# An attention block in one pass: the first batch's values multiplied early, the other batches' values from half-precision parts

## The reference

```python
out = bilinear_resize(x, 64, 64)
out = relu(bn(conv1x1(out, conv1_w), bn1_s, bn1_b))
q, k, v = conv1x1(out, q_w, q_b), conv1x1(out, k_w, k_b), conv1x1(out, v_w, v_b)
energy = einsum('bdi,bdj->bij', q, k)            # q, k: 32 channels, 4096 points
out = gamma * einsum('bcj,bij->bci', v, softmax(energy)) + out
out = relu(bn(out, bn2_s, bn2_b))
out = bilinear_resize(bn(conv1x1(out, conv2_w), bn3_s, bn3_b), 128, 128)
return relu(out + x)
```

## Time and profile before

| | us |
|---|---|
| median of 3 runs (2367.70 to 2368.66) | 2367.78 |
| the profiled execution, whole | 2371.97 |
| its span in the trace | 2370.2 |
| first batch: entry until the first product of the blocks | 0 to 144.3 |
| second batch: entry | 624.4 to 708.1 |

### The profile page before, as it was taken

The page is one execution under the profiler, slowest core; times in us unless marked ns, Lnnn a source line. Parts: engine busy times, 40 slices in busy tenths (PEclk is TensorE's granted clock), DMA queues, the critical chain, the costliest instruction groups (busy, mean ns, idle before and its releaser), DMA issues.

```text
span 2370.2 us, 48197 instructions
## 1 busy us (share of the span) xinstructions
PE 2298.5 (97%) x15970; PEld 1650.3 (70%) x15970; DVE 1783.7 (75%) x3294; ACT 1706.3 (72%) x3305; POOL 1671.0 (70%) x1610
## 2 busy tenths in 40 slices
PE   4799999999999999999999999999999999999998
PEld 2377777777667777777747777777775777777774
DVE  7666578887568888888657888888756777777778
ACT  5567777777657777777755777777765777777773
POOL 7992468888369988888728988889845454444464
PEclk8899999999999999999999999999999999999999
DMA  6321112322102332222301322233310112222322
GB/s 212 107 72 46 36 54 107 106 92 104 54 23 103 108 107 103 93 105 98 107 10 54 109 106 102 102 107 106 106 55 1 63 63 71 71 71 71 142 96 100
DMA packets 59273, 204.11 MB, mean 86 GB/s; under 512 B 8752, under 2 KB 9840, under 8 KB 59120
## 3 DMA queue, kind: packets, MB, share of 16 engines
q1 hardware_dynamic: 41696, 138.93, 18.2%
q10 hardware_dynamic: 17424, 63.45, 6.5%
HBM read 135.24 MB, written 67.11 MB: 85 GB/s over the span
## 4 chain that ended last, share of the span: by engine, by line
PE 88%; DVE 4%; ACT 3%; POOL 3%; issue 1%; SPq 1%; DMA 0%; DVEq 0%; ACTq 0%; POOLq 0%
PE acc L1139 19%; PE acc L1141 18%; PE acc L1140 18%; PE et L1015 10%; PE emx L1003 6%; PE wrk L1037 4%; PE acc L1065 4%; PE wrk L1003 3%; PE acc L1057 2%; PE wrk L1028 1%; DVE qs L768 1%; DVE ks L768 1%; PE acc L1049 1%; ACT qs L535 1%; ACT qs L534 1%
## 5 line engine op out<-in xcount | busy, mean ns | idle before, releaser
L1139 PE MATMUL acc<-vh,ph 128*128 128x257 f16 x4096 | 1120.1, 273 | 1.7 <-DVE vl L778 1.4
L1141 PE MATMUL acc<-vh,pl 128*128 128x257 f16 x4096 | 1116.2, 273 | 0.0
L1140 PE MATMUL acc<-vl,ph 128*128 128x256 f16 x4096 | 1110.9, 271 | 0.0
L463 ACT ACTIVATE ph<-et 128x512 f16<-128x512 f32 x1024 | 610.5, 596 | 301.8 <-PE et L1015 293.0
L727 DVE TENSOR_TENSOR pl<-et,ph 128x512 f16<-128x512 f32 x1024 | 700.6, 686 | 139.4 <-ACT et L464 135.8
L464 ACT ACTIVATE et<-et 128x512 f32<-128x512 f32 x1024 | 607.0, 593 | 0.0
L1140 PEld LDWEIGHTS acc<-vl,ph 128*128 128x128 f16 x4096 | 400.9, 98 | 277.4 <-issue 20.5
L1139 PEld LDWEIGHTS acc<-vh,ph 128*128 128x128 f16 x4096 | 400.2, 98 | 70.6 <-issue 11.0
L1141 PEld LDWEIGHTS acc<-vh,pl 128*128 128x128 f16 x4096 | 395.4, 97 | 56.2
L377 POOL TENSOR_TENSOR ct<-cd,uw 128x512 f32<-128x512 f32 x246 | 325.0, 1343 | 134.7 <-DVE xres L758 130.3
L1015 PE MATMUL et<-qs,ks 98*128 (+1 forms) x1024 | 390.2, 381 | 2.7 <-DVE pl L727 0.9
(11 more groups left out here) (142 smaller groups left out, 2673.0 us busy)
## 6 DMA issues: line engine op xcount, KB each, us to landing
xres<-in_x SPq DMA_DIRECT2D x139, 512.0 KB, 4.5
out<-xres ACTq DMA_DIRECT2D x121, 512.0 KB, 2.6
xin<-in_x SPq DMA_DIRECT2D x110, 512.0 KB, 3.7
xr<-in_x SPq DMA_DIRECT2D x7, 512.0 KB, 7.4
out<-xr SPq DMA_DIRECT2D x6, 512.0 KB, 2.6
out<-xr SPq DMA_DIRECT2D x2, 256.0 KB, 2.1
osb<-in_L_conv_conv_w SPq DMA_DIRECT2D x1, 256.0 KB, 7.7
osb<-in_L_conv_v_w SPq DMA_DIRECT2D x1, 256.0 KB, 7.8
```

The costliest lines, as they stand in the source:

```text
L463: ops.activation(ph[:, t % 4, :], et[t % 2][:, :], ACT.Exp)
L1139: mm(acc[it][:, 0:C + 1], ph[:, tt % 4, pt], vh[:, tt, 0:C + 1], start=tt == 0, stop=False)
L1140: mm(acc[it][:, 0:C], ph[:, tt % 4, pt], vl[:, tt, :], start=False, stop=False)
L1141: last = mm(acc[it][:, 0:C + 1], pl[:, tt % 4, pt], vh[:, tt, 0:C + 1], start=False, stop=tt == JT - 1)
```

## The change

In the first batch, v0 to v13 are multiplied between the steps of the convolution: the two values of chunk k-1, v(2k-2) and v(2k-1), stand behind c(2k+1) and the m that follows it. As the scale isn't known yet, ACT copies each result in float32 into `xr`, over rows that the convolution has used (`keep_values`). After q7, ACT makes the eight high parts of 1024 columns each from these copies (`kept_high`), and DVE the low parts: two in the entry, six in the steps 1, 3, 5, 7, 9 and 11 of the first block (`kept_low`). POOL writes a chunk of `xr` for the next batch only after its values were multiplied.

In the other batches the values' operands are split into half-precision parts: ACT and DVE split `a` (scaled) chunk by chunk into `a_high` and `a_low`, again kept in `xr`, and PE multiplies 12 half-precision matmuls for each v. The scale of `a` comes from the size of the batch's small image, which DVE reads in eight reductions in the last block of the batch before (`largest_z`), from sums on PE at step 29, and from constants made once in block 1 (`fixed_sizes`).

```diff
+        def a_part(ck, low, half):
+            return xr[:, ck].rearrange("p h r c -> p (h r c)").bitcast(F16)[:, (low * CH + half) * IB:(low * CH + half + 1) * IB]
+        def kept(ck):
+            return xr[:, ck].rearrange("p h r c -> p (h r c)")
...
 (SP, last block)
-                    sp.wait_ge(c1_rdy, 2 * NB * B)
+                    sp.wait_ge(v_rdy, VU * B)
...
 (POOL, blk)
+                        if j == 0:
+                            pool.wait_ge(v_rdy if b else v_done, b * VU + 2 * (n + 1))
...
 (ACT)
+            def a_high(b, ck):
+                if ck == 0:
+                    act.wait_ge(a_rdy, b)
+                for half in range(CH):
+                    last = ops.activation(a_part(ck, 0, half), a[:, half, ck * IB:(ck + 1) * IB], ACT.Copy,
+                                          scale=a_scale[:, half:half + 1])
+                last.then_inc(a_hi, 1)
+            def keep_values(v):
+                act.wait_ge(v_rdy, v + 1)
+                ops.activation(kept(v // 2)[:, v % 2 * VB * C:(v % 2 + 1) * VB * C], acc[bank_of(0, "values", v)][:, :],
+                               ACT.Copy).then_inc(v_kept, 1)
+            def kept_high(ck):
+                if ck == 0:
+                    act.wait_ge(vscale, 4)
+                act.wait_ge(v_kept, 2 * ck + 2)
+                ops.activation(vh[:, ck * IT:(ck + 1) * IT, 0:C], kept(ck).rearrange("p (j c) -> p j c", c=C), ACT.Copy,
+                               scale=vg[:, 2:3]).then_inc(vh_rdy, 2)
...
 (DVE)
+            def a_low(b, ck):
+                dve.wait_ge(a_hi, (b - 1) * NB + (ck + 1))
+                for half in range(CH):
+                    last = ops.scalar_tensor_tensor(a_part(ck, 1, half), a[:, half, ck * IB:(ck + 1) * IB],
+                                                    a_scale[:, half:half + 1], a_part(ck, 0, half), ALU.mult, ALU.subtract)
+                last.then_inc(a_lo, 1)
+            def largest_z(b, ck):
+                dve.wait_ge(down_p, down_count(b + 1, PIECES * (ck + 1)))
+                ops.tensor_reduce(z_max[:, ck, :], xr[:, ck].rearrange("p h r c -> p h (r c)"), AX.X, ALU.max,
+                                  apply_absolute_value=True).then_inc(z_seen, 1)
+            def kept_low(ck):
+                dve.wait_ge(vh_rdy, 2 * ck + 2)
+                js = slice(ck * IT, (ck + 1) * IT)
+                ops.scalar_tensor_tensor(vl[:, js, :], kept(ck).rearrange("p (j c) -> p j c", c=C), vg[:, 2:3], vh[:, js, 0:C],
+                                         ALU.mult, ALU.subtract).then_inc(v_done, 2)
...
 (PE, values)
+                        if not is_first(b):
+                            high, low = (a_part(jt // IT, i, h)[:, keys] for i in range(2))
+                            mm(out, high, wvh[:, h, :], start=h == 0, stop=False)
+                            mm(out, high, wvl[:, h, :], start=False, stop=False)
+                            last = mm(out, low, wvh[:, h, :], start=False, stop=h == CH - 1)
+                            continue
...
 (PE, step 29 of a batch's last block)
+                        for h in range(CH):
+                            last = mm(wrk[:, C + 1:C + 2], ones_p[:, :], z_all[:, h:h + 1], start=h == 0, stop=h == CH - 1)
+                        last.then_inc(z_sum, 1)
...
+def _first_sequence(engine):
+    seq, kept = [], [("kept", ck) for ck in range(NB)]
+    for ck in range(NB):
+        m = [("max", u) for u in range(IT * (ck - 2), IT * (ck - 1))] if ck >= 2 else []
+        first, second, middle = [("conv1", 2 * ck)], [("conv1", 2 * ck + 1)], [("qk", ck - 1)] if ck else []
+        v = [("values", i) for i in range(2 * ck - 2, 2 * ck)] if ck else []
+        if engine == "V":
+            seq += first + second + m[:3] + middle + m[3:]
+        else:
+            seq += first + m[:2] + middle + m[2:3] + second + m[3:] + v
...
+T_KEPT = (1, 3, 5, 7, 9, 11)
+T_Z = (1, 3, 7, 10, 12, 19, 20, 26)
```

More of the change, by code:

```diff
@@ L552, in enter @@
                         conv1_out(b, i // 2, i % 2)
+                        if i % 2 and not is_first(b):
+                            act.wait_ge(c1_done, b * (2 * NB) + (i + 1))
+                            a_high(b, i // 2)
                         if i == 1 and not is_first(b):
@@ L557, in enter @@
                         qk_high(b, i)
+                    elif kind == "values" and is_first(b):
+                        keep_values(i)
+                    elif kind == "kept":
+                        kept_high(i)
                     elif kind == "values":
@@ L787, in enter @@
                         qk_low(b, i)
+                    elif kind == "a_low" and not is_first(b):
+                        a_low(b, i)
                     elif kind == "max":
@@ L851, in blk @@
                         pair_max(b, n + 1, units[0])
+                    if g == 1 and t == T_FIXED:
+                        fixed_sizes()
+                    if c == NB - 1 and b < B - 1:
+                        if t in T_Z:
+                            largest_z(b, T_Z.index(t))
+                        if t == T_Z[-1]:
+                            size_of_z(b)
+                        if t == T_SIZE + 1:
+                            size_of_a(b)
+                    if g == 0 and t in T_KEPT:
+                        kept_low(2 + T_KEPT.index(t))
                     if c > 0 and t in (T_OT[0] + 1, T_OT[1] + 1):
@@ L1166, in blk @@
                         shift_transposes(g + 1)
+                    if c == NB - 1 and t == T_SIZE and not (isinstance(b, int) and b == B - 1):
+                        pe.wait_ge(y_rdy, g * 2)
+                        pe.wait_ge(z_rdy, b + 1)
+                        for h in range(CH):
+                            last = mm(wrk[:, C + 1:C + 2], ones_p[:, :], z_all[:, h:h + 1], start=h == 0, stop=h == CH - 1)
+                        last.then_inc(z_sum, 1)
+                        if is_first(b):
+                            pe.wait_ge(a_size, 1)
+                            for h in range(CH):
+                                last = mm(wrk[:, C + 2:C + 4], ones_p[:, :], a_parts[:, h, :], start=h == 0, stop=h == CH - 1)
+                            last.then_inc(a_sum, 1)
             def batch(b):
@@ L1217 @@
 PAR_OPS = 5
+def _first_sequence(engine):
[8 more added lines that the diff above has]
+            seq += first + m[:2] + middle + m[2:3] + second + m[3:] + v
+    m = [("max", u) for u in range(EU - 2 * IT, EU)]
+    v = [("values", i) for i in range(VU - 2, VU)]
+    row, one, scale, qk, shift, rows = (("bound_row", 0), ("bound_all", 0), ("scale", 0), ("qk", NB - 1), ("shift", 0),
+                                        ("shift_rows", 0))
+    energies = [("energies", i) for i in range(3)]
+    if engine == "V":
+        return seq + [row, m[0], m[1], one, scale, m[2], qk, *m[3:], kept[0], rows, kept[1], *energies]
+    if engine == "A":
+        return seq + [qk, *v, *kept, *energies]
+    return seq + [m[0], m[1], row, qk, one, m[2], m[3], v[0], m[4], m[5], v[1], m[6], m[7], shift, *energies]
 def _sequence(vector):
@@ L1227, in _sequence @@
         first, second, middle = [("conv1", 2 * ck)], [("conv1", 2 * ck + 1)], [("qk", ck - 1)] if ck else []
-        seq += first + second + m[:3] + middle + m[3:] if vector else first + m[:2] + middle + m[2:3] + second + m[3:]
+        low = [("a_low", ck - 1)] if ck else []
+        seq += first + second + m[:3] + middle + m[3:] + low if vector else first + m[:2] + middle + m[2:3] + second + m[3:]
     m = [("max", u) for u in range(EU - 2 * IT, EU)]
@@ L1232, in _sequence @@
     if vector:
-        seq += [row, m[0], m[1], one, scale, m[2], qk, v[0], m[3], m[4], m[5], v[1], m[6], v[2], m[7], *v[3:6]]
+        seq += [row, m[0], m[1], one, scale, m[2], qk, v[0], m[3], m[4], m[5], v[1], m[6], v[2], m[7], ("a_low", NB - 1), *v[3:6]]
     else:
@@ L1247, with ring_of, bank_of @@
 A_SEQUENCE.insert(A_SEQUENCE.index(("qk", NB - 1)) + 1, ("values", 0))
[L1248 removed]
+FIRST_SEQUENCE, V_FIRST, A_FIRST = (_first_sequence(e) for e in "PVA")
+FIRST_RING, RING = ([x for x in q if x[0] in ("conv1", "qk", "values")] for q in (FIRST_SEQUENCE, SEQUENCE))
 assert [RING.index(("values", VU - IT + i)) % IT for i in range(IT)] == list(range(IT))
[L1252 to L1253 removed]
+def ring_of(b):
+    return FIRST_RING if isinstance(b, int) and b == 0 else RING
+def bank_of(b, kind, i):
+    return ring_of(b).index((kind, i)) % 4
 AHEAD = 3
```

114 lines of the change are left out of this document (91 added, 23 removed).

## The result

The changed kernel takes 2386.8 us (median of 4 runs, 2384.0 to 2388.5) against 2368.2 (4 runs, 2367.7 to 2368.7): a ratio of 1.0073, 95% interval 1.0061 to 1.0086, some 17 us slower. The forecast was 2375.0, in a range of 2360 to 2384. The direction was right, and the size was off by more than half.

What follows compares the result with a forecast made beforehand. PE bounds the kernel, busy 2298.5 of 2370.2 us, except in the first batch's head, a chain of load, ACT, DVE and PE. First batch +6.4, later batches −1.3, constants +2.2: +7.3 on 2367.78 gives 2375.0 us, range 2360 to 2384.

Steps and rivals of the forecast that it cites:

- The head: First batch's entry: ACT's copies delay the weighted rows, turns of 15.5 us instead of 11.8, c14 at 117.3.
- the 2.5: First batch's head: a stop of PE lowers its clock and costs 2.5 us beyond itself.
- A: The forecast itself: head turns of 15.5 us, clock falling at stops; 2375.0 us, range 2369 to 2382; chance 0.47.
- B: First batch's head: same circle of waits, but the clock stays up, turns of 13.0 us; 2365 us; chance 0.22.
- ACT's high parts: End of the first batch's entry: eight high parts of 1024 columns, 1.03 us each, 8.3 us in all.
- block 0's loss of clock: Start of block 0: PE stands over 6 us before it, so the low clock costs 2.5 us.
- The gain of the tail: Later batches, v7 to v15: half-precision values save 0.41 us for each of nine units, 3.7 us per batch.
- The failed step: Convolution of batches 1 to 3: splits fit DVE's idle 2.5 us per chunk, meeting POOL at odd chunks; +0.6 per batch.
- D: Convolution of later batches: DVE's low parts wait for POOL, 1.1 us per chunk, 22 us, taken as +13; 2388; chance 0.12.
- fixed_sizes: Block 1, step 2: 3.8 us of DVE work between two differences that PE waits for; +2.2 us (0 to 4).
- largest_z: Last block of the batch before: eight reductions of 1.3 us hidden in 15 us of DVE idle time; without cover 10.
- C: Head: copies don't hold up weighted rows, loads come late and POOL alone sets c14 at 101.4; 2359 us; chance 0.13.

Runs made afterwards that it cites:

- e9: Changed kernel with ACT's copies behind the weighted rows, fixed_sizes split over three steps, last two chunks' low parts later in DVE's queue; ratio 0.9950 to before.
- e3: Changed kernel without DVE's low parts in batches 1 to 3, PE multiplying the high part in their place; ratio 0.9961 to the kernel before.
- after: The changed kernel itself, with all parts of the change, against the kernel before; 2386.8 us, ratio 1.0073.
- e4: Changed kernel with all edits of the later batches taken out, only the first batch's part left; ratio 1.0008 to the kernel before.

## Why the forecast was right in the sign and wrong in the size

- **The head** (turns of 15.5, c14 at 117.3, first product at 148.1): in the profiled run m14, c14 and the first product came out within 1.2 us. As a mean it is too dear. I had added the 2.5 to every turn; the six profiles show turns of 12.9 as well as 14.2 to 15.8, and the part alone costs 1.9 us by its runs, not 6.4. A and B were not exclusive: the clock falls in some turns.
- **ACT's high parts** (8.3 us) measured 8.4, and block 0's loss of clock (+2.5) measured 1.5 (52.0 against 50.5). The six low parts in block 0 (+0.7) cost nothing: with the clock kept, block 0 takes what it took before.
- **The gain of the tail** (9 x 0.41 = 3.7 a batch) measured 3.7 to 3.8 (11.3 for three), with the splits in it. Without the low parts it is 5.6, so they take 1.8 there, near the 0.9 and 0.7 that I allowed.
- **The failed step** is the convolution of batches 1 to 3: "In the convolution the splits go into 2.5 us of DVE idle time per chunk ... at the odd chunks they meet POOL ...; +0.6." Measured were +5.8, +7.6 and +4.1. It was a sum of idle time, where the place in the queue decides. The 7.6 of the third batch holds 1.7 of slow clock at its start, which is no low part's. DVE's idle time was ahead of the queries' low parts, waiting for ACT; a pair stretched to 2.6 us makes it late for them, 0.8 us at each of two chunks, and a_high 0.4 at the first. At the last chunk one more pair stood ahead of row, and PE waited 1.51 and 1.65 us where it waits 0.7 and 0.3 without the low parts: 2.1 us, of which 0.8 stand behind a stretched pair (e9 keeps them) and 1.3 behind the pair ahead of row (e9 is rid of them). In the fourth batch that was all: 0.4 + 0.8 + 0.8 + 2.1 = 4.1. In the second the low clock that followed made 2.8 of the 2.1 and another 1.0 behind q7. D named this place and POOL as the cause; its price of 22 us was not far from the 16.2 that e3 shows, and I gave it 0.12. That its 2388 lies next to the measured 2386.8 is luck in part: it has the stretch at every chunk and nothing more for the pair ahead of row, and its other terms are the forecast's.
- **fixed_sizes** (+2.2) measured +5.0. I let it compete with differences only. What was late was the residual behind it, and through ACT's queue a product of the maxima; 3.4 us of idle time and 1.6 of clock.
- **largest_z** was hidden: the last block of batches 0 to 2 is 0.6, 0.3 and 0.2 us longer, and the sum at step 29 with its small operations (+0.7) is in that.
- A slip of the sum: −2.1 + 0.45 + 0.6 + 0.7 is −0.35 a batch, so three batches are −1.1 and not −1.3. By its own terms the forecast was 2375.3.
- C's ground (the load as last releaser, POOL behind it) was weak for this kernel: the weighted rows stood behind the copies, not behind the load. Only with the copies moved does the load come last again, and the turns of 12.0 us came back at once.

By the runs, e4 puts 1.9 us on the first batch's part and leaves 15.4 to the others, give or take 3.6. The profiles of after and e4 give 12.3 for these without the head and block 0: 4.8 in block 1, 6.2 in the entries and 1.4 in other blocks. The difference lies within the interval.

## What to carry to other kernels

An engine's idle time in a stage is not room for new work: look at what it waits for when idle, and at what is due right behind the new work, stretched by whoever shares its port. When work is added to an engine that closes a circle, its place in the queue decides and not its length; here the same two copies cost 9 to 12 us more ahead of the weighted rows than behind. And an engine that merely relays, as ACT did between the residual and the maxima, belongs in the list of what waits.
